# Local attention: row sums of the odd heads by one VectorE instruction instead of with ScalarE's exponentials

## What is computed

```python
for l in range(2):                                   # DEPTH
    h = shift_token(x)
    q, k, v = jnp.split(h @ wqkv[l], 3, axis=-1)     # 8 heads of 64
    q, k = l2norm(q) * q_scale[l], l2norm(k) * k_scale[l]
    q, k = rotary_xpos(q, k)
    sim = jnp.einsum('bhwid,bhwjd->bhwij', q * 8, look_around(k))
    attn = jax.nn.softmax(jnp.where(mask, -big, sim), axis=-1)
    x = x + merge(jnp.einsum('bhwij,bhwjd->bhwid', attn, look_around(v))) @ wo[l]
    x = x + gated_mlp(layernorm(shift_token(x)))
```

## Time and profile before

| | |
|---|---|
| median of 3 runs | 2631.54 us (2631.46 to 2634.67) |
| profiled execution | 2637.19 us, of which the span 2635.6 us |
| PE busy | 2543.2 us (96%) |
| ACT busy | 2155.1 us (82%) |
| DVE busy | 2005.9 us (76%) |
| POOL busy | 1665.7 us (63%) |
| exponentials of local attention (L1037) | 1024, 460.0 us in all, and 1024 reads of the accumulator, 235.9 us |

### The profile page before, as it was taken

One profiled execution on the slowest core, in us unless ns is written; L12 is line 12 of the kernel. 1 busy time (PEld: TensorE's weight loads), 2 busy tenths in 40 slices (PEclk: granted clock), 3 DMA queues, 4 the chain that ended last, 5 costly groups with the idle time before them and its releaser, 6 DMA issues.

```text
span 2635.6 us, 71253 instructions
## 1 busy us (share of the span) xinstructions
PE 2543.2 (96%) x24208; PEld 1991.5 (76%) x24208; DVE 2005.9 (76%) x5640; ACT 2155.1 (82%) x6334; POOL 1665.7 (63%) x1974
## 2 busy tenths in 40 slices
PE   6999999999999999999899899998998999999899
PEld 4777777777777777777678788887786888888777
DVE  4667666667666666666589899998568999999865
ACT  5888888888888888888589899999447999999844
POOL 3544444444444444444489889998237999999743
PEclk9999999999999999999999999999899999999999
DMA  2000000000000000000112311111201111111121
GB/s 74 6 13 9 10 5 9 6 9 9 10 5 9 5 10 10 9 6 5 38 37 46 101 38 38 42 40 30 70 17 41 44 43 38 43 38 41 27 69 53
DMA packets 131878, 76.13 MB, mean 29 GB/s; under 512 B 83700, under 2 KB 114240, under 8 KB 131520
## 3 DMA queue, kind: packets, MB, share of 16 engines
q1 hardware_dynamic: 122896, 67.31, 10.7%
q10 hardware_dynamic: 8624, 4.27, 0.6%
HBM read 16.99 MB, written 8.41 MB: 10 GB/s over the span
## 4 chain that ended last, share of the span: by engine, by line
PE 45%; issue 2%; POOL 1%; DVE 1%; ACT 1%; SPq 1%; DMA 0%; DVEq 0%; POOLq 0%; ACTq 0%
PE bank L1275 5%; PE bank L1241 5%; PE bank L1254 5%; PE bank L1206 4%; PE bank L1297 4%; PE bank L1220 4%; PE bank L1207 3%; PE bank L1208 3%; PE bank L1449 3%; PE bank L1229 2%; PE bank L1440 2%; PE bank L1441 2%; PE bank L1442 2%; PE bank L866 1%; POOL f_qkr L981 1%
## 5 line engine op out<-in xcount | busy, mean ns | idle before, releaser
L319 POOL TENSOR_SCALAR L<-L,rinv 128x128 f32<-128x128 f32 (+3 forms) x1024 | 525.5, 536 | 599.4 <-DVE rinv L511 599.4
L391 ACT ACTIVATE L<-L,nmax 128x384 f32<-128x384 f32 (+3 forms) x1024 | 572.9, 563 | 139.7 <-DVE nmax L497 139.7
L497 DVE CUSTOM_DVE_ANT_0 L<-bank,f_rows 128x256 f32<-128x256 f32 (+3 forms) x1024 | 470.3, 479 | 171.9 <-PE bank L613 170.1
L1037 ACT ACTIVATE f_L<-bank,f_nmax,f_rn 128x128 f32<-128x128 f32 x1024 | 460.0, 483 | 4.3 <-DVE f_nmax L1162 4.2
L999 POOL TENSOR_TENSOR f_rn<-f_ssq,f_mhalf 128x16 f32<-128x16 f32 x128 | 419.1, 3274 | 20.4 <-DVE f_ssq L1146 7.2
L981 POOL TENSOR_TENSOR f_qkr<-f_rows 128x256 f32<-128x256 f32 x512 | 417.0, 845 | 22.1 <-DVE f_rows L1113 22.1
L634 PE MATMUL bank<-ident,L 128*128 128x128 f32 x2560 | 370.3, 276 | 2.3 <-DVE PT L216 2.0
L634 PEld LDWEIGHTS bank<-ident,L 128*128 128x128 f32 x2560 | 297.9, 141 | 82.7 <-issue 44.9
L1113 DVE TENSOR_TENSOR f_rows<-bank,f_rows 128x512 f32<-128x512 f32 x512 | 348.0, 680 | 8.3 <-ACT f_sq L1027 8.3
L655 PE MATMUL bank<-PT,v 128*64 128x512 f32 (+3 forms) x2048 | 303.9, 439 | 0.6 <-DVE yacc L532 0.4
L655 PEld LDWEIGHTS bank<-PT,v 128*64 128x64 f32 x2048 | 126.8, 136 | 165.9 <-issue 164.6
(11 more groups left out here) (157 smaller groups left out, 6461.0 us busy)
## 6 DMA issues: line engine op xcount, KB each, us to landing
f_vm<-f_v SPq DMA_DIRECT2D x224, 128.0 KB, 2.4
xb<-in_L_attn_x SPq DMA_DIRECT2D x16, 256.0 KB, 2.9
out<-yacc SPq DMA_DIRECT2D x32, 128.0 KB, 1.8
f_hs<-xf SPq DMA_DIRECT2D x128, 32.0 KB, 1.9
out<-f_acc ACTq DMA_DIRECT2D x16, 256.0 KB, 2.3
f_hs<-xf SPq DMA_DIRECT2D x128, 28.0 KB, 1.8
L<-bias_rows SPq DMA_DIRECT2D x4, 512.0 KB, 7.5
f_hs<-xf SPq DMA_DIRECT2D x128, 3.8 KB, 1.9
```

Source lines behind the costliest of these rows:

```text
L319: nc.gpsimd.tensor_scalar(t, t, rinv[:, h % RING, a, i:i + 1], 1.0, ALU.mult, ALU.mult).then_inc(s_N, 1)
L391: nc.scalar.activation(t, t, ACT.Exp, bias=nmax[:, ep % RING, a, i:i + 1], scale=-1.0, accum_out=rsum[:, ep % RING, a, i:i + 1]).then_inc( ...
L497: nc.vector.tensor_tensor_reduce(out=L[:, p % RING, a, LOFF[i]:LOFF[i] + (i + 1) * P], in0=ps_s[a][i], in1=bias_tab[:, 2 * p + a, T - (i + ...
L1037: nc.scalar.activation(L[:, ot % 2, a, k, :], ps_s[a][:, k * P:k * P + P], ACT.Exp, bias=nmax[:, ot % 2, a, k:k + 1], scale=rn[:, ot % 2, ...
```

## The change

The exponentials of the odd heads no longer have an `accum_out`; those of the even heads keep it. In DVE's slot a new `tensor_reduce` stands between `sums(1)` and the odd heads' reciprocals. It waits until the four odd exponentials of its tile are done (`exp_odd`), sums the four rows of 128 of `L` into `rsum` in one instruction, and counts a new semaphore, `osum`, for which DVE waits before the reciprocal reads `rsum`. No instruction that is kept changes its place.

```diff
@@ scalar: exps(a, tile)
                 for k in range(FC):
+                    how = {"accum_out": rsum[:, ot % 2, 0, k:k + 1]} if a == 0 else {}
                     nc.scalar.activation(L[:, ot % 2, a, k, :], ps_s[a][:, k * P:k * P + P], ACT.Exp,
                                          bias=nmax[:, ot % 2, a, k:k + 1], scale=rn[:, ot % 2, 2 * k + a:2 * k + a + 1],
-                                         accum_out=rsum[:, ot % 2, a, k:k + 1]).then_inc(sem[("exp_even", "exp_odd")[a]], 1)
+                                         **how).then_inc(sem[("exp_even", "exp_odd")[a]], 1)
...
@@ vector: slot(b, t)
             sums(1, two)
+            if four is not None:
+                tb, tt = four
+                dve.wait_ge(sem["exp_odd"], at(tb, FC * TT, FC * tt + FC))
+                nc.vector.tensor_reduce(rsum[:, tt % 2, 1, :], L[:, tt % 2, 1], AX.X, ALU.add).then_inc(sem["osum"], 1)
+                dve.wait_ge(sem["osum"], at(tb, TT, tt + 1))
             inverse(1, four)
```

More of the change, by code:

```diff
@@ L1481 @@
 ATTN_SEMS = ["hs0", "hs1", "hs2", "hs3", "weights", "tab", "w_hi", "w_lo", "hT_done", "hT_hi", "hT_lo", "q_done", "k_done", "v_done",
-             "v_out", "q_squared", "k_squared", "ssum", "ssq", "rn", "q_products", "k_products", "q_rotated", "k_rotated", "kr", "qT_done", "qT_out", "kT_done",
+             "v_out", "q_squared", "k_squared", "ssum", "ssq", "osum", "rn", "q_products", "k_products", "q_rotated", "k_rotated", "kr", "qT_done", "qT_out", "kT_done",
              "kT_out", "scores_even", "scores_odd", "rmax", "nmax", "exp_even", "exp_odd", "rinv_even", "rinv_odd", "probs_even", "probs_odd",
```

## The result

The changed kernel takes 2675.56 us (median of 4 runs, 2672.43 to 2678.27) against 2632.22 us of the kernel before measured with it: a ratio of 1.0163, 95% interval 1.0145 to 1.018. It is slower by 43 us; 2670.5 was predicted, inside a range of 2656 to 2716.

A forecast was written before the change was run, and what follows sets the result against it. Bound: a 7.85 us slot loop through DVE and POOL, as tight as PE's own work. Adding 0.32 a slot over 118 slots, plus the layer ends, gives +39 us: 2631.5 + 39 = 2670.5, range 2656 to 2716.

The forecast's parts named there:

- The loop: Local attention slot through DVE and POOL: `f_rn` to first rotation 3.26, to key scaling's end 2.67, to next `f_rn` 1.92.
- Reduction: New `tensor_reduce` on DVE between `sums(1)` and the odd reciprocal, inside the loop: 0.67 us a slot.
- Wait for `osum`: DVE's wait between the reduction's end and the odd reciprocal: 0.03 us, with 0.17 kept for the range.
- the 0.37: Part of `f_ssq`'s 0.54 us on DVE taken as a wait for POOL's port, given back after the change.
- What comes behind keeps its distances: After a short `f_ssq`, the odd product starts 0.08 later, `f_rn` 0.17 later, and `f_rn` still takes 3.29 us.
- The key scaling is pinned: DVE's key scaling (L1182) ends about 2.67 us after the first rotation, held by POOL's third rotation, not DVE's queue.
- ACT: Dropping four odd-head accumulator reads frees 4 x 0.09 = 0.36 us a slot on ACT, off the deciding path.
- One is PE's own work: Of two loops as long as the 7.85 us slot, one was PE's work, back to back without idle time.
- Rival 2: PE's work covers the addition through hidden slack in the DVE and POOL loop: slot 7.85, 2631 to 2636 us; chance 0.09.
- rival 1: The port wait of `f_ssq` is not given back, 0.70 enters the loop: slot 8.55, 2714 us; chance 0.12.
- rival 3: ACT is the true bound, so its relief makes the kernel faster: 2602 to 2625 us; chance 0.03.
- rival 4: Gaps in every slot make PE's granted clock fall to 1.2 GHz for stretches: over 2720 us; chance 0.03.

The follow-up runs named there:

- `one_head`: Changed kernel with only one of the four odd heads reduced on DVE, the other three keeping their accumulator reads: 2632.9 us, ratio 1.0004.
- `before_half_product`: Kernel before, with POOL's even product (L990) on 64 of the 128 columns of each head: 2666.42 us, ratio 1.013.
- the cuts: Kernel before with POOL's even product on 64 of 128 columns (2666.42 us), or DVE's odd product on 4 of 128 (2666.1 us).
- `half`: Changed kernel with two of the four odd heads reduced on DVE, the other two keeping their accumulator reads: 2643.8 us, ratio 1.0049.
- `neither`: Kernel before without the odd heads' accumulator reads and without any reduction, odd reciprocals taken of the even heads' sums: 2631.11 us, ratio 0.9998.
- `half_ahead`: Changed kernel with two of the four odd heads reduced on DVE, the reduction standing ahead of `sums(1)`: 2632.52 us, ratio 1.0001.
- `behind_ssq`: Changed kernel with the reduction, its wait and the odd reciprocals moved behind `f_ssq`, ahead of the odd product: 2713.45 us, ratio 1.0306.
- `before_small_odd`: Kernel before, with DVE's odd product (L1151) on 4 of the 128 columns of each head: 2666.1 us, ratio 1.0124.

## Why the prediction was right

- *The loop.* 3.26 + 2.67 + 1.92 before; in the changed kernel 3.31 (1699.33 to 1702.64) + 2.68 (to 1705.32) + 2.22 (to 1707.54) = 8.21, against 8.17. Its third piece was forecast at 1.92 + 0.33 = 2.25 and its first as unchanged; the errors of the two, -0.03 and +0.05, partly cancel.
- *The terms.* Reduction 0.67, measured 0.67. Wait for `osum` 0.03, measured 0.04 (1707.17 to 1707.21). `f_ssq` 0.17, measured 0.16, and `one_head` and `before_half_product` show by its length that the 0.37 was a port wait. The reciprocal to `f_ssq` 0.12, measured 0.09.
- *What was missed in size.* "What comes behind keeps its distances" was off by 0.05: the odd product stands 0.12 behind `f_ssq`, not 0.08, holds the port into `f_rn` that much longer, and `f_rn` lasts 3.34. 118 x 0.04 = 5 us, about the distance from +39 to +43. Behind a short `f_ssq` the product hangs on the odd reciprocal, and starts 0.03 after its end in the changed kernel (1707.39 to 1707.42) and in the layer's last slot alike. `f_ssq` came 0.03 nearer to the reciprocal (0.09, not 0.12), `f_rn` with it, and the product did not.
- *The key scaling is pinned.* It ends 2.68 after the first rotation with an issue 1.57 after it. Right in the band where it was used, but it holds only for an issue in the third rotation; in the fourth it is 3.37, as the cuts showed.
- *ACT.* 0.36 a slot was predicted, 0.37 measured (1.37 instead of 1.74 for four), and it is worth nothing. The Trainium skill (ScalarE: Activation LUTs, "What ACT_TABLE_LOAD costs"), which the prediction set beside it, gave 0.2; the trace's spacing without a read is 0.34, not the 0.386 worked out from that page.
- *How much of the span.* In the two profiles the first to last `f_ssq` of a layer takes 18.8 and 20.8 us longer, the rest of the program 3.4 us less, 36 in all; the medians differ by 43, since the profiled execution of the kernel before lies 5 us above its median and that of the changed one 2 us below. The layers' 39.6 is close to the forecast's 39 in part by luck: the 116 regular distances grew by 0.36 each, 41 us, and not 0.32; the first three of each layer and the two where a DMA was late became 2.5 us shorter in all, where the forecast had nothing for the first and a growth for the last.
- *Wrong in the prediction.* "One is PE's own work": PE had at least 0.05 us of slack, hidden in records that leave no gap. `half` shows the same: PE at 100.00 of 100 with a slot of 7.94. It did no harm, since the other loop decided. Rival 2 (PE covers it) rested on it and falls with the slot of 8.21, rival 1 with `f_ssq`'s 0.16, rival 3 with `neither`, rival 4 with the clock of 1.00. One sign did not come: POOL was to be idle before L990 too, and waits 0.16 there as before (0.15).

## What to carry to other kernels

When several engines are 95 to 100% busy, look for loops: follow one result round until it comes back to its own engine, and add up the pieces between issue and issue. An instruction costs what it adds to the longest loop, less any wait inside that loop that it fills (0.37 here), and a move out of one loop is worth nothing if the new place lies in another. Where two engines share a port, the time depends on which instruction is issued during which, so that taking work away can cost as much as adding it: after any shift, look at the length of each instruction that was not touched.

No variant that scales all probabilities by their own sums beat the kernel before. `one_head` and `half_ahead` equal it within their intervals, and show that about 0.3 us a slot of other work would be free on DVE at this place.

## What the runs showed of the hardware beyond what was expected

- An accumulator read on ScalarE lasts 0.19 to 0.26 us and delays the next instruction by 0.09.
- A DVE product with both inputs in SBUF waits while POOL runs a rotation (1.11 instead of 0.68), and so does a 128x8 instruction (`f_nmax`, 0.65 instead of 0.17). A 128x16 `tensor_scalar` (`f_ssq`, 0.54 instead of 0.17) waits while POOL runs its product. The power `f_rn` on POOL, 2.9 us long, does not hold a product or `f_nmax` up: in the kernel before `f_nmax` takes 0.17 in the midst of it, and in `behind_ssq` the odd product is issued 0.76 after `f_rn` starts and takes its usual time.

```profile
1704.19 0.69 DVE L1157 TENSOR_TENSOR f_L<-f_L,f_rinv 128x512 f32<-128x512 f32 x1
```

It waits itself, though, when a DVE product is ahead of it (3.29 to 3.34 instead of the 2.91 of `before_small_odd`). The Trainium skill (SBUF — State Buffer, "SBUF: two separate sides") has the port held for the whole instruction by whoever comes first; the trace agrees for the rotations and the products, and not for the power.
- `tensor_reduce` beside POOL's product keeps its length (0.65 and 0.67 in the changed kernel), as the Trainium skill says of it (SBUF — State Buffer, "Who interferes with whom").
- Transposes that wait for their input cost PE about the wait, and no more. In the changed kernel their weight loads wait 0.41 for the key scaling and the next projection's load sits idle another 0.24, but the four loads take 0.42 instead of 0.59: from their start to the next load it is 0.67, against 0.65 in the kernel before (the last two rows below).

```profile
1705.37 0.42 PEld L1226 LDWEIGHTS bank<-ident,f_qkr 128*128 128x128 f32 x4 [0.41 <-DVE f_qkr L1188]
1706.04 0.19 PEld L1212 LDWEIGHTS bank<-f_wv_hi,f_hT_hi 128*128 128x128 f32 x1 [0.24 <-issue]
...
1707.77 0.59 PEld L1220 LDWEIGHTS bank<-ident,f_qkr 128*128 128x128 f32 x4
1708.42 0.19 PEld L1206 LDWEIGHTS bank<-f_wv_hi,f_hT_hi 128*128 128x128 f32 x1
```
